# A six-stage decoder on one core: the ternary stage's inner norm applied behind its second product, one context laid out transposed in DRAM, and norms and weights of a stage made in the stage in front

## The reference

```
h = x @ sign-rounded(W_fc).T        # 256 -> 1024, weights in {-1, 0, 1} by their mean magnitude
h = gelu(h)
h = (h - mean(h)) / sqrt(var(h) + eps) * ln_w + ln_b      # over the 1024, the inner norm
out = h @ sign-rounded(W_proj).T    # 1024 -> 256
```

## Time and profile before

| | us |
|---|---|
| median of three executions | 1425.71 |
| the profiled execution, its own time | 1422.83 |
| its span, first to last instruction | 1420.9 |
| PE busy in the span | 1329.2 (94%) |
| DVE, ACT, POOL busy | 1001.7, 782.4, 371.4 |
| first work of b, c, a1, a2, d | 281.6, 420.5, 668.5, 924.6, 1229.0 |
| ACT copy 128x512 from PSUM (L194), from SBUF (L1732); gelu 128x512 (L1717) | 0.60, 0.63, 0.59 |
| 16 fold matmuls 128x256 f32 in the tail of a0 (L413), first start to next work | 264.90 to 268.35 |
| PE waits for row maxima in a1, group 15; for exp in a2, group 15 | 1.9; 1.3 |
| PE waits for exp in b, 395 to 415 us | 2.2, in two waits |
| cast L1542 in c: the first, the median | 0.70, 0.37 |
| a load of 512 KB of weights, issue to landing | 4.3 |
| granted clock of PE, mean of the span | 0.983 |

### The profile page before, as it was taken

How to read it: one execution, slowest core, us unless ns; L and a number is a source line. 1 busy time by engine, 2 the same in 40 slices (tenths; PEclk the granted TensorE clock), 3 DMA queues, 4 the chain that set the end, 5 groups by cost and what they waited for, 6 DMA issues and landing times. The chain is left out here.

```text
span 1420.9 us, 41741 instructions
## 1 busy us (share of the span) xinstructions
PE 1329.2 (94%) x15796; PEld 1197.8 (84%) x15796; DVE 1001.7 (70%) x2423; ACT 782.4 (55%) x1569; POOL 371.4 (26%) x458
## 2 busy tenths in 40 slices
PE   5999999799979999998999999889999999689887
PEld 5889889699969999998898999768888888578777
DVE  5888888455554545453777777677777777788885
ACT  2655555355545445453555565545555556377786
POOL 1212212011111212110000000055555555134442
PEclk9999999899989999999999999999999999899999
DMA  6000000031000000001000000020000000000000
GB/s 228 3 2 0 0 0 3 7 113 36 30 31 1 1 0 0 0 1 32 22 3 0 0 0 1 2 84 17 16 15 15 15 8 2 1 16 22 30 23 30
DMA packets 16477, 28.72 MB, mean 20 GB/s; under 512 B 3616, under 2 KB 7712, under 8 KB 16000
## 3 DMA queue, kind: packets, MB, share of 16 engines
q1 hardware_dynamic: 16384, 27.44, 5.9%
HBM read 23.24 MB, written 4.19 MB: 19 GB/s over the span
## 5 line engine op out<-in xcount | busy, mean ns | idle before, releaser
L830 DVE TENSOR_REDUCE a_row_max<-a_S 128x4 bf16<-128x512 f32 (+1 forms) x384 | 246.8, 683 | 54.4 <-PE a_S L993 28.8
L723 ACT ACTIVATE a_probs<-a_S 128x512 f32<-128x512 f32 x384 | 208.9, 595 | 112.8 <-PE a_S L1006 60.3
L172 POOL TENSOR_TENSOR all_var_eps<-all_moments,all_ln_eps 128x2 f32<-128x2 f32 x96 | 25.1, 262 | 714.7 <-DVE all_moments L167 714.7
L961 PE MATMUL a_S<-a_qm_hi,all_odd_split 32*128 32x256 f32 x1536 | 187.8, 302 | 7.3 <-DVE a_row_max L830 4.2
L961 PEld LDWEIGHTS a_S<-a_qm_hi,all_odd_split 32*128 32x128 f32 x1536 | 131.5, 183 | 41.5 <-issue 26.2
L687 POOL TENSOR_TENSOR a_shifts<-a_add_mask,a_row_max 128x512 bf16<-128x512 bf16 x128 | 131.0, 1040 | 118.1 <-DVE a_row_max L830 118.1
L952 PE MATMUL a_S<-all_odd_split,a_qm_hi 32*128 32x128 f32 x1536 | 126.8, 283 | 1.7 <-DVE all_odd_weights L938 1.7
L180 DVE TENSOR_SCALAR all_xn<-all_x_res,all_moments,all_rstd 128x256 f32 (+1 forms) x192 | 99.8, 561 | 19.6 <-POOL all_rstd L174 18.8
L961 PE MATMUL a_S<-a_qm_lo,all_odd_split 32*128 32x256 f32 x768 | 108.7, 277 | 0.0
L1019 PE MATMUL a_AV<-a_probs,a_v_pad 128*32 128x128 f32 x3072 | 103.8, 276 | 0.0
L952 PEld LDWEIGHTS a_S<-all_odd_split,a_qm_hi 32*128 32x128 f32 x1536 | 99.8, 185 | 2.6 <-DVE all_odd_weights L938 2.5
(11 more groups left out here) (250 smaller groups left out, 3865.9 us busy)
## 6 DMA issues: line engine op xcount, KB each, us to landing
all_cx<-in_ctx SPq DMA_DIRECT2D x32, 256.0 KB, 2.8
all_x_res<-in_x SPq DMA_DIRECT2D x8, 512.0 KB, 7.7
out_x<-all_x_res SPq DMA_DIRECT2D x16, 256.0 KB, 2.0
b_routed_wi<-in_L_ffn_wi_W SPq DMA_DIRECT2D x1, 1024.0 KB, 5.2
b_routed_wo<-in_L_ffn_wo_W SPq DMA_DIRECT2D x1, 1024.0 KB, 8.0
all_even_weights<-in_L_ffn_W_fc SPq DMA_DIRECT2D x1, 1024.0 KB, 4.9
all_even_weights<-in_L_ffn_W_proj SPq DMA_DIRECT2D x1, 1024.0 KB, 6.9
a_a_raw<-in_L_attn_Wqkv SPq DMA_DIRECT2D x1, 512.0 KB, 4.3
```

Of the source, the lines that this page charges most:

```text
L723: act.activation(probs[:, t % STEPS, :], S2[t % 2][:], ACT.Exp, scale=DH ** -0.5).then_inc(exp_ok, 1)
L830: dve.tensor_reduce(row_max[:, t % 4, :], S1[t % 2][:].rearrange("p (h k) -> p h k", h=QH), AXX, ALU.max).then_inc(max_ok, 1)
L961: pe.matmul(S2[t % 2][:, c * HV * P:(c + 1) * HV * P], k[par][strip, c, tok], q[par][strip, c, b].rearrange("p h t -> p (h t)"), start=(c ...
```

## The change

1. **Ternary stage.** The mean and rstd of the inner norm are applied to the output of the second product. POOL multiplies the gelu output by a row of gains (`scale_hidden`, 4 passes of 128x512 per window), PE turns the scaled hidden layer of the window before without waiting for its moments, ACT takes the high part straight from PSUM, DVE all four low parts. The output is x + offset_sum + rstd * (OUT - mean * gain_sum): POOL adds the constant (`add_offset`), DVE does two passes for each of two sequences (`add_output`). The two sums are made once, by 16 fp32 matmuls in window 0. x is normalised by ACT (`act_normalise`), with -mean*rstd from POOL. A load of the gain row (128x1024) is issued at the stage's start.
2. **Entangled stage.** The context comes transposed from DRAM; no PE transposes; ACT takes the high part and POOL the low part out of SBUF. The loads wait for POOL's low part instead of PE's transposes.
3. **Tail in front.** Stages a0, b and a2 also prepare group 1 of the next stage's norm. Next weights start at G = 13 instead of 15 (the entangled weights stay at 15); the small matmul goes to bank FA, and the values product of G = 13 waits until the level is read from it. The gelu table is loaded in a2 at step 2 of group 16, and the first two gelus of window 0 come before x of window 1 is split.

```diff
 class GroupNorm:
+    def pool_offset(self, pool, w):
+        pool.tensor_tensor(self.offset[:], self.moments[:, :, 0], self.minus_one[:], ALU.mult).then_inc(self.minus_ok, 1)
+        pool.wait_ge(self.rstd_ok, w + 1)
+        pool.wait_ge(self.minus_ok, w - 1)
+        pool.tensor_tensor(self.offset[:], self.offset[:], self.rstd[:], ALU.mult).then_inc(self.offset_ok, 1)
+
+    def act_normalise(self, act, w):
+        act.wait_ge(self.offset_ok, w - 1)
+        at_least(act, self.full, w)
+        for b in range(PAIR):
+            last = act.activation(self.xn[:, b, :], self.x(w, b), ACT.Identity, bias=self.offset[:, b:b + 1],
+                                  scale=self.rstd[:, b:b + 1])
+        last.then_inc(self.xn_ok, 1)
...
 class SplitWeights:
+        self.first = NG - 3
...
 class TernaryWeights(SplitWeights):
+    def act_slot(self, act, slot, banks):
+        super().act_slot(act, slot, banks)
+        if slot == (NG - self.first) * STEPS + 2:
+            act.activation(self.first_gelu[:], self.ones[:, 0:1], ACT.Gelu)
+    def wait_taken(self, pe):
+        pe.wait_ge(self.level_ok, 1)
...
 def attention_stage(...):
+                    if second_of_next(G) and t == 3:
+                        dve.wait_ge(out_free, 2)
+                        next_norm.dve_moments(dve, 1)
...
-                    if isinstance(G, int) and G >= NG - 1:
-                        following.dve_slot(dve, (G - NG + 1) * STEPS + t, NEXT_BANKS)
+                    if isinstance(G, int) and G >= following.first:
+                        following.dve_slot(dve, (G - following.first) * STEPS + t, next_banks(G))
...
 def entangled_stage(...):
+                if in_stage(w + 1):
+                    pool.wait_ge(c_hi, w + 2)
+                    at_least(pool, vt_full, w)
+                    context.pool_low(pool, 1 - parity, cT_hi[1 - parity], cT_lo[1 - parity]).then_inc(c_lo, 1)
...
-                    act.wait_ge(pc_full, w + 2)
-                    act.activation(cT_hi[1 - parity][:], chunked(PC), ACT.Copy).then_inc(pc_hi, 1)
+                    at_least(act, vt_full, w)
+                    context.act_high(act, w + 1, 1 - parity, cT_hi[1 - parity]).then_inc(c_hi, 1)
...
-                    dve.wait_ge(pc_hi, w + 2)
-                    dve.tensor_tensor(cT_lo[1 - parity][:], chunked(PC), f32(cT_hi[1 - parity][:]), ALU.subtract).then_inc(pc_lo, 1)
...
-                            last = pe.transpose(PC[:, c * TOK + b * P:c * TOK + (b + 1) * P],
-                                                cx[1 - parity][:, b, c * P:(c + 1) * P], consts["ident"][:])
...
 def ternary_stage(...):
         def _(pool):
             def window(w, parity):
                 if has_norm(w):
                     norm.pool_rstd(pool, w + 2)
+                    norm.pool_offset(pool, w + 2)
+                if in_stage(w):
+                    scale_hidden(w, 0, parity)
+                    scale_hidden(w, 1, parity)
                 if in_stage(w - 1):
-                    low_part(pool, w - 1, 0, 1 - parity)
-                if in_stage(w - 1):
-                    low_part(pool, w - 1, 1, 1 - parity)
+                    add_offset(w - 1)
                 if in_stage(w):
+                    scale_hidden(w, 2, parity)
+                    scale_hidden(w, 3, parity)
...
         def _(act):
             def window(w, parity):
+                if starts(w):
+                    activate(w, 0, parity)
+                    activate(w, 1, parity)
                 ln.act_high(act, w, parity, hb_full, FILLS)
...
                     if in_stage(w - 1):
-                        rescale(w - 1, n, 1 - parity)
+                        high_part(w - 1, n, 1 - parity)
+                    if has_norm(w) and n == 1:
+                        norm.act_normalise(act, w + 2)
...
         def _(dve):
+            def add_output(w, parity):
+                dve.wait_ge(out_full, w + 1)
+                dve.wait_ge(hrstd_ok, w + 1)
+                dve.wait_ge(biased, w + 1)
+                for b in range(PAIR):
+                    dve.scalar_tensor_tensor(OUT[:, b * D:(b + 1) * D], minus_sum[:], h_moments[parity][:, b, 0:1],
+                                             OUT[:, b * D:(b + 1) * D], op0=ALU.mult, op1=ALU.add).then_inc(centred_ok, 1)
+                for b in range(PAIR):
+                    dve.wait_ge(centred_ok, w * PAIR + b + 1)
+                    last = dve.scalar_tensor_tensor(norm.x(w, b), OUT[:, b * D:(b + 1) * D], h_rstd[parity][:, b:b + 1],
+                                                    norm.x(w, b), op0=ALU.mult, op1=ALU.add)
+                last.then_inc(out_ok, 1)
             def window(w, parity):
+                if takes_moments(w):
+                    dve.wait_ge(norm.xn_ok, w + 2)
+                    norm.dve_moments(dve, w + 2)
                 ln.dve_low(dve, w, parity)
                 if in_stage(w):
                     spread(w, 0, parity)
                     spread(w, 1, parity)
+                if in_stage(w - 1):
+                    low_part(w - 1, 0, 1 - parity)
+                if in_stage(w - 1):
+                    low_part(w - 1, 1, 1 - parity)
...
                 if in_stage(w - 2):
-                    dve.wait_ge(out_full, w - 1)
-                    dve.tensor_tensor(norm.x_group(w - 2), norm.x_group(w - 2),
-                                      OUT[:].rearrange("p (b d) -> p b d", b=PAIR), ALU.add).then_inc(out_ok, 1)
-                if has_norm(w):
-                    norm.dve_normalise(dve, w + 2)
+                    add_output(w - 2, parity)
...
         def _(pe):
             def turn(w, n, parity):
+                pe.wait_ge(scaled_ok, w * FILLS + (FILLS if n >= PARTS // 2 else FILLS - 1))
+                at_least(pe, ylo_ok, (w - 1) * PARTS + n + 1)
```

More of the change, by code:

```diff
@@ L1635, in routed_stage, with ternary_stage @@
     return nm
-def ternary_stage(nc, name, before, norm, consts, wt, out_dram, next_norm=None):
+def ternary_stage(nc, name, before, norm, consts, wt, out_dram, spare, gain_dram, next_norm=None):
     FC = F // P
@@ L1720, in rescale @@
[L1720 to L1728 removed]
+                act.activation(half_of(hid[parity], n), HB[n % 2][:], ACT.Gelu).then_inc(gelu_ok, 1)
```

245 lines of the change are left out of this document (139 added, 106 removed).

## The result

The changed kernel takes 1392.32 us, median of five executions (1392.18 to 1396.39), beside 1424.56 for the kernel before (1423.34 to 1426.29): ratio 0.9775, 95% interval 0.9762 to 0.9788. It saves 32.2 us; the forecast was 1400.0 with a range of 1393 to 1410, so the side was right and the gain was larger than the range allowed, by 0.7 us at the median. The profiled executions compare as 1422.8 and 1392.2, their spans as 1420.9 and 1390.1: 30.8 us, against the 25.7 of the prediction's sum.

A forecast was written before the change was run, and what follows sets the result against it. The ternary window was taken as bound by x arriving late from DVE beside POOL, with PE the bound afterwards. Terms of 14.2 + 0.8 + 0.8 + 4.5 + 4.7 + 0 + 0.4 + 0.3 = 25.7 us off 1425.7 gave 1400.0, range 1393 to 1410.

The forecast's parts named there:

- The rest: Small closing terms: routed norm made in the entangled tail 0.4 us, query/key split moved to group 13 0.3, memset and semaphores 0.
- One more memset [...]: 0: Across the kernel: one added memset and more semaphores to clear stand beside waits and cost 0 us.
- Ternary windows: Windows 2 to 13 of the ternary stage: period falls from 11.23 to 10.05 us with PE the bound, 14.2 us saved.
- Ternary start: First ternary matmul to window 2: 19.55 us becomes 15, weight sums of 3.4 filling a hole; 4.5 us saved.
- Last windows and drain: End of the ternary stage: windows 14 and 15 save 0.8 us, the drain's shorter chain another 0.8.
- Entangled stage: Entangled windows: four context transposes leave PE, 0.36 us each window over 13 windows, 4.7 us saved; bounds 0 and 5.8.
- Weights in the tail in front: Second cross attention: preparing ternary weights earlier gains 5.7 us at its end, costs 6.0 in groups 13 and 14; sum zero.
- Rival 1: Cross attention group 14: each of eight quantising passes waits out a POOL shift, price 4 to 6 us, kernel 1405; chance 0.16.
- the prediction's second reading: Cross attention, by the skill's shared-port rule: all eight quantising passes and POOL's shifts block each other fully; kernel about 1405 us.
- 2 (10.7 a window): Ternary window stays bound by a chain, slow POOL passes and x late behind ACT's queue; 8 us, kernel 1408; chance 0.14.
- 4 (POOL): Ternary stage: POOL passes of 2.2 us make POOL the bound, kernel 15 us slower than before, 1441; chance 0.03.
- 3 (better): Group 14 hides the quantising in DVE's idle time and the ternary start keeps its clock; kernel 1394 us; chance 0.09.

The follow-up runs named there:

- e1: Kernel before the change plus three unused tiles that shift addresses as in the changed kernel, no instruction differing; 1419.74 us, ratio 0.9957 to the kernel before.
- e3: Changed kernel with unused tiles moving the weights by 32 bytes and the stages' tiles by 128; 1398.22 us, ratio 0.9808 to the kernel before.
- e8: Changed kernel with fillers and longer weight rows, so every SBUF tile and weight row starts at a multiple of 128 bytes; 1399.66 us.
- e6: Changed kernel with the 16 float32 weight-sum matmuls made as 32 float32r ones on high and low column parts; 1386.76 us, ratio 0.9739.
- e7: Changed kernel with a sixth 128x512 POOL multiply per ternary window, into a tile nothing reads; 1392.58 us, ratio 0.9759 to the kernel before.
- e2: Changed kernel with an unused tile behind the norm buffers, moving the stages' tiles by 32 bytes; 1396.60 us, ratio 0.9792 to the kernel before.
- e4: Changed kernel with ternary x normalised by DVE again, behind its window's output passes, instead of by ACT; 1419.96 us, ratio 0.9953 to the kernel before.
- e10: Changed kernel with all tiles and weight rows at multiples of 128 bytes, plus 64 bytes between weights and tiles; 1391.2 us.
- e12: Changed kernel with all tiles and weight rows at multiples of 128 bytes, plus 64 bytes ahead of the weights and 64 behind; 1391.1 us.
- e9: Changed kernel with ternary x normalised by DVE between the window's first and second low parts, instead of by ACT; 1406.20 us, ratio 0.9873.

## Why the prediction was wrong, and what in it held

The side and the mechanism in the ternary window held. What failed is the sum: 25.7 forecast, 30.8 measured in the profiled executions. The step that failed first of all is the one in "The rest" that put the new tiles at nothing ("One more memset [...]: 0"). The addresses that they shift gave 4.1 us in the routed stage, shown by e1, which is most of the 5.1 missing (step 6). The changed kernel with the slow addresses, e3 and e8, takes 1398.22 and 1399.66, beside the 1400.0 forecast. That this comes so near is partly luck: inside the ternary stage the windows were sized 3.4 us too low and the start and the end together 4.4 too high, and these cancel. Step by step:

**1. Ternary windows: right mechanism, undersized.** 14.2 forecast, 17.6 measured: 12 x (11.23 - 9.77). The period was taken at 10.05, PE's own work of 9.9 and up to 0.2 of waiting. PE never waits for ACT's x, and its work is 9.77 at most, less than I had read from the slices of the earlier trace rows. POOL's passes came at 1.29 for 1.2 taken.

**2. Ternary start: the term that was mis-sized the other way.** 4.5 forecast, 2.3 measured. I priced the sums at 3.4 us, from the fold's "16 matmuls" in the table. Those 16 are records of 8 calls in the code, so a float32 matmul shows here as two records (the line on the fold in the table ahead of the prediction counts records); the change makes 16 calls, 32 records, 6.72 us. Per call it is 0.43 us in the fold and 0.42 here. And I called them hidden. e6 shows that they lie on PE's path. The Trainium skill (FP8 and Floating Point Precision, TensorE Precision Notes) gives a true float32 product four passes through the array. The traces roughly agree: 6.72/16 = 0.42 is 3.6 times the 0.117 of one float32r matmul of e6.

**3. Last windows and drain.** 1.6 forecast, -0.6 measured (from window 14 to the end 37.4 before, 38.0 after). The output bank is emptied behind two low parts in the last window, a wait of 2.1 us in the timeline of PE, and the last 32 matmuls take 5.58 us at a mean granted clock of 0.70, so in part at the lower level:

```profile
1380.22 5.58 PE L1930 MATMUL d_OUT<-all_even_split,all_odd_split 128*128 128x256 f32 x32 [2.11 <-DVE all_x_res L1851]
```

**4. Entangled stage: right.** 4.7 forecast, 4.0 measured. The period fell from (395.73 - 293.92)/13 = 7.83 to (389.32 - 292.60)/13 = 7.44, by 0.39 for 0.36; at the stage's end 1.0 was lost with `b_OUT` at a granted clock of 0.50 for 0.90 (2.07 us for 1.14).

**5. Weights in the tail in front: zero was too low.** The gain came out smaller (2.9 of 5.7, and 1.4 in e7's trace), but the bill of 6.0 was mostly not presented: one group grew by 0.7. "21.1 against 17.75, so 3.4 us late" took the seven passes as if all had to be paid in one group; DVE runs full across groups 14 and 15 and PE loses 2.3 us. Rival 1 said that each pass waits out a shift. None did; one waited for POOL's bias add (1.09 us from 1176.91, the add running from 1176.36). The four passes that compare and subtract met shifts, each starting 0.16 to 0.17 us ahead of one (as 1184.20 to 1184.37), and there POOL waited: timeline of POOL in the changed kernel, each row two shifts or one, of which one took 2.0 us in place of 1.04.

```profile
1178.68 3.01 POOL L738 TENSOR_TENSOR a_shifts<-a_add_mask,a_row_max 128x512 bf16<-128x512 bf16 x2 [1.23 <-DVE a_row_max L883]
...
1184.37 2.01 POOL L738 TENSOR_TENSOR a_shifts<-a_add_mask,a_row_max 128x512 bf16<-128x512 bf16 x1 [2.68 <-DVE a_row_max L883]
```

So the prediction's second reading, that these passes and POOL's exclude each other, was right. It didn't say which engine would pay, and here it was mostly POOL, which had time to spare.

**6. Routed stage: the term put at nothing, and the step that failed.** 0.4 forecast, 4.4 measured, and by e1 4.1 of it from addresses. "One more memset [...]: 0" is where it was lost: it priced the instruction and not the tile. The edit's three new tiles (a constant, and an offset for each of the two norm buffers) shift everything allotted behind them, by 32 bytes for the weights and 96 for the stages' tiles.

**7. Tails.** 1.4 us at the end of a0 went unforeseen. The last products of a0 before and after, in the timeline of PE:

```profile
275.78 2.93 PE L104 MATMUL a_FA<-all_odd_split 128*128 128x256 f32 x12 [0.93 <-DVE all_odd_split L843]
```

```profile
275.64 1.70 PE L104 MATMUL a_FA<-all_odd_split 128*128 128x256 f32 x12 [0.93 <-DVE all_odd_split L896]
```

Same work, at a granted clock of 0.50 and of 1.00; before them PE had been idle by turns in both. No run isolates this. From the start to b the changed kernel's experiments, whose first stage has the same instructions, take from 280.1 us (e6) to 284.6 (e2), so the 1.4 gained here is within what executions differ by. The 1.1 us of a1 and the norm of group 1 made in front weren't separated either, and the entangled part alone wasn't tried.

The rivals: 2 (10.7 a window) and 4 (POOL) are ruled out, by the period and by e7: even six passes a window cost next to nothing (9.84 for 9.77). 3 (better), at 1394, came true in both its conditions, quantising mostly hidden and the start at the full clock, but the start gave less than it counted on, and the place of the tiles gave what it didn't. What none of them said is that x could have been late in DVE's queue (e4), the slower case that this change really stood next to.

## What to carry to other kernels

Price a matmul by calls and by the operand type, not by counting records of a group, and ask of one-off work in a pipeline's first window whether another engine is really still busy while it runs. A pass that moves to a less loaded engine must be looked at in both ways, where it stands in the old queue and what it meets there; the one cost 25 to 28 us here, the other 14. When a kernel is bound by PE, compare matmul spacing stage by stage after every edit that adds a tile: tiny unused tiles moved this kernel by 4 to 6 us, and a change may be praised or blamed for that. And read the clock of a stage's tail in several traces before giving it to a change: here the same code ended at 1.00 in one and at 0.66 in another.

## What the hardware did unexpectedly

- The rate of 128x256 float32r matmuls hung on where their operands lie in SBUF: 113.5 to 120 ns for the same product (`c_OUT`), depending on 32 or 64 bytes in the place of either side. Both operands at multiples of 128 (e8) gave the slow rate. Another product of the same shape (`c_HB`) hardly reacted: 278 or 279 for 285 ns per matmul in half the windows of e10 and e12.
- Where a DVE pass and a POOL pass excluded each other, mostly the one that started later paid: DVE 0.41 to 1.39 us in e9, POOL 1.04 to 2.0 in the cross attention. But a POOL pass that follows another at once can go ahead of a DVE pass that is already waiting. In e9 the first pass of a normalisation starts at 1276.83, in the last 0.1 us of one multiply, and takes 1.50 us: it also stands out the next multiply, which starts at 1276.89.
- POOL can be busy 97% in a loop (e7) and add only 0.07 us to its period.
